# Layer 2 attention: value products in three steps of a round, projections in the other five

## The chip, the cores and the metric

The kernel runs on one NeuronCore of a Trainium2 chip. Its time is the device time of one launch in microseconds (us); lower is better. TensorE does the matrix products, VectorE and ScalarE work on their results in PSUM, GpSimd does small elementwise work, and SyncE's queue starts the loads. The engines run their own instruction streams in order and meet at semaphores.

## The reference, cut to what matters

Four layers, each a cross attention and a feed-forward part. The change touches the attention of layer 2 alone (8 batches, 256 queries, 512 keys, 16 heads of width 64, all in float32):

```python
def _L2_xattn_ref(x, context, mask, Wq, Wkv, Wout, b_out):
    HEADS, DIM_HEAD = 16, 64
    SCALE = DIM_HEAD ** (-0.5)
    q = x @ Wq.T
    k, v = jnp.split(context @ Wkv.T, 2, axis=-1)
    ...
    sim = jnp.einsum('bhid,bhjd->bhij', q, k) * SCALE
    sim = jnp.where(mask[:, None, None, :], sim, max_neg)
    attn = jax.nn.softmax(sim, axis=-1)
    out = jnp.einsum('bhij,bhjd->bhid', attn, v)
    return out.transpose(0, 2, 1, 3).reshape(B, Nq, HEADS * DIM_HEAD) @ Wout.T + b_out
x = x + _L2_xattn_ref(_layernorm(x, axis=-1), ctx_1024, mask_BxS2_bf1, ...)
```

## The kernel before, in words

`wide_attention` works on one batch at a time. The 16 heads are 8 pairs; a **round** is the 4 pairs of one half of the heads, so a batch has two rounds and the layer 16 (n = 2b + r). A round has eight **steps**, one for each block of 32 queries (QB = 8); a batch has steps s = 0 to 15, of which 0 to 7 are its first round and 8 to 15 its second. Below, "step two of a round" is the second one, s % 8 == 1.

In a step each engine does the following, in the order in which it is written for that engine:

- **TensorE** first issues the scores of the step that comes next (`scores`, L2007: 8 matmuls of a 64-row, 32-column tile, for two PSUM banks `s_ps`), after `max_ready` says that VectorE has read the scores before them. Then it fills banks for the step's **jobs** (`fill`): K, Q and V projections of this or the next batch (L1988, L1986, L1373), the turning XT of the normed input (L1982), and the output product OUT of the batch before (L1993, 8 matmuls). All jobs take turns in two PSUM banks, `ring` (RING = 2); a bank is refilled when `m.drained` says that it was emptied. Last come value products of the round before (`outputs`, L2023): 16 blocks of 32 keys, 8 matmuls each on 32-row, 64-column tiles, into `pv_ps`. With the last blocks go 8 matmuls (L2029) that spread the inverses of the softmax sums over the other half of `pv_ps`.
- **VectorE** takes the masked negative maxima of the scores of the next step (`maxima`, L1797, two), turns the probabilities of this step in 32x32 blocks (`turn_probs`, L1809, two), and in step one of a round multiplies `pv_ps` by its inverses (`normalise_outputs`, L1822) and inverts the sums of the round just ended (`invert_sums`, L1816). It also drains OUT jobs and takes their moments.
- **ScalarE** takes the exponentials for the next step (`exponentials`, L1926, two), in step one of a round copies the spread inverses from `pv_ps` to `o` (`copy_inv`, L1936), and then drains the step's K, Q, V and XT jobs from the ring (L1910, L1908, L1912, L1906).

Which job stands in which step is written in tables: `this_batch`, `next_batch`, `last_batch`, and `end_values` and `for_local` for the end of the last batch, where LOCAL jobs belong to the feed-forward part that follows. `blocks_of` says which of the 16 blocks of value products stand in which step of a round: before, seven of the eight steps have two or three. The value products of a round need `normalise_outputs` of the round before them (`m.pv_copied`), since they write the same `pv_ps`.

Of the kernel before, what the change touches and what calls it, by code (L numbers as in the profile page):

```python
# [41 lines left out]
class Ring:  # L42
# [15 lines left out]
    def bank(self, u, m):  # L58
        return self.banks[self.index(u, m)]
# [1436 lines left out]
class FirstLocal:  # L1496
# [3 lines left out]
    SHIFT, TURN, QK, V = 0, 1, 2, 2 + 2 * TPB  # L1500
# [123 lines left out]
def wide_attention(m):  # L1624
# [10 lines left out]
    QB, KB = S // BLK, KV // BLK  # L1635
# [4 lines left out]

    XT, Q, K, V, OUT, LOCAL = range(6)
    NQ, NV = NG // 2, 2 * CPB
    this_batch = {0: [(K, 4), (K, 5), (K, 6)], 1: [(K, 7)], 2: [(Q, 2)], 3: [(Q, 3)], 4: [(V, 0)], 5: [(V, 1)], 6: [(V, 2)], 7: [(V, 3)],
                  14: [(V, 4), (V, 5)], 15: [(V, 6), (V, 7)]}
    next_batch = {7: [(XT, 0)], 8: [(K, 0), (K, 1), (K, 2)], 9: [(K, 3)], 11: [(Q, 0)], 13: [(Q, 1)]}
    last_batch = {10: [(OUT, 0)], 12: [(OUT, 1)]}
    end_values = {8: [(V, 4), (V, 5)], 9: [(V, 6), (V, 7)]}
    for_local = {10: [0], 11: [1], 12: [2], 13: [3], 14: [4], 15: [5]}
    blocks_of = {1: range(0, 3), 2: range(3, 6), 3: range(6, 8), 4: range(8, 10), 5: range(10, 12), 6: range(12, 14), 7: range(14, 16)}

    def step_jobs(b, s):
        end = b + 1 == B
        jobs = [(f, b - 1, n) for f, n in last_batch.get(s, ()) if b > 0]
        own = end_values if end and s >= QB else this_batch
        jobs += [(f, b, n) for f, n in own.get(s, ()) if b > 0 or f == Q]
        jobs += [(f, b + 1, n) for f, n in next_batch.get(s, ()) if not end]
        if end:
            jobs += [(LOCAL, b, n) for n in for_local.get(s, ())]
        return jobs
    before = [(XT, 0, 0), (Q, 0, 0), (Q, 0, 1)]  # L1660
    steps = {(b, s): step_jobs(b, s) for b in range(B) for s in range(STEPS)}
    behind = [(LOCAL, B - 1, 6), (LOCAL, B - 1, 7), (OUT, B - 1, 0), (OUT, B - 1, 1)]
    jobs = before + [job for b in range(B) for s in range(STEPS) for job in steps[b, s]] + behind
    number = {job: n for n, job in enumerate(jobs)}

    with ExitStack() as ctx:
# [39 lines left out]
        def ahead(b, s):  # L1706
            return (b, s + 1) if s + 1 < STEPS else (b + 1, 0)

        with nc.Block() as block:
# [55 lines left out]
            def _(dve):  # L1765
# [92 lines left out]
                for b in range(B):  # L1858
                    for s in range(STEPS):
                        n = ROUNDS * b + s // QB  # L1860
                        if ahead(b, s)[0] < B:
                            maxima(*ahead(b, s))
                        turn_probs(b, s)
                        if s % QB == 0 and n >= 2:
                            normalise_outputs(n - 2)
                        if s % QB == 0 and n >= 1:
                            invert_sums(n - 1)
                        for job in steps[b, s]:
                            drain(job)
                        if s == 13 and b > 0:  # L1870
                            out_moments(b - 1)
                        if s == 15 and b > 0:
                            out_scale(b - 1)
                        if s == 6 and b + 1 < B:
                            convert_mask(b + 1)
                        if s == 10 and b + 2 < B:
                            scale(b + 2)
                        if b + 1 == B and s == 9:
                            dve.wait_ge(*m.out_normed.after(2 * TPB))
                            local.copy_half(dve)  # L1880
                            local.tables(dve)
                        if b + 1 == B and s == 14:
                            local.sum_squares(dve, 0)
# [14 lines left out]
            @block.scalar  # L1898
            def _(act):
                def drain(job):  # L1900
                    f, b, n = job
                    if f == OUT:
                        return
                    act.wait_ge(*full(job))
                    if f == XT:
                        ins = act.activation(xnT[b % 2][:], bank(job)[:, 0:S], ACT.Copy)  # L1906
                    if f == Q:
                        ins = act.activation(q[:, 2 * n:2 * n + 2, :].rearrange("p g s -> p (g s)"), bank(job)[:], ACT.Copy, scale=hd ** -0.5)  # L1908
                    if f == K:
                        ins = act.activation(kT[:, n, :], bank(job)[:], ACT.Copy)  # L1910
                    if f == V:
                        ins = act.activation(first.place_values(n), bank(job)[:], ACT.Copy)  # L1912
                    if f == LOCAL:
                        ins = local.drain(act, n, bank(job))
                    ins.then_inc(drains(job), 1)
                    if f == LOCAL and n in (local.QK + 1, local.QK + 3):
                        local.square(act, (n - local.QK) // 2, empty_local)

                def exponentials(b, s):
                    r, qb = divmod(s, QB)  # L1920
                    if qb == 0 and ROUNDS * b + r >= ROUNDS:
                        act.wait_ge(*m.sums_inverted.after(ROUNDS * b + r - 1))
                    for w in range(2):
                        n = 2 * s + w
                        act.wait_ge(*m.max_ready.after(UNITS * b + n + 1))
                        act.activation(probs[n % 4][:], probs[n % 4][:], ACT.Exp, bias=nmax[:, b % 2, n:n + 1], scale=-1.0,  # L1926
                                       accum_out=sums[:, r, w, qb:qb + 1]).then_inc(m.probs_ready.sem, 1)

                def copy_inv(n):

                    b, r = divmod(n, ROUNDS)
                    act.wait_ge(*m.pv_done.after(n + 1))
                    if b >= 1:
                        for j in range(TPB):
                            act.wait_ge(*full((OUT, b - 1, j)))
                    act.activation(o[:, NC * r:NC * (r + 1), :], pv_ps[:, :, S:2 * S], ACT.Copy).then_inc(m.inv_copied.sem, 1)  # L1936

                for job in before:
                    drain(job)
                exponentials(0, 0)  # L1940
                for b in range(B):
                    for s in range(STEPS):
                        n = ROUNDS * b + s // QB
                        if ahead(b, s)[0] < B:
                            exponentials(*ahead(b, s))
                        if s % QB == 0 and n >= 2:
                            copy_inv(n - 2)
                        for job in steps[b, s]:
                            drain(job)
                copy_inv(LAST - 1)  # L1950
                for job in behind[0:TPB]:
                    drain(job)
                copy_inv(LAST)
# [1616 lines left out]
```

## Time and profile before

| | |
|---|---|
| median of 3 runs | 1759.72 us (1755.17 to 1760.15) |
| the profiled execution | 1760.41 us, its span 1758.5 us |
| mean granted TensorE clock | 0.926 |
| TensorE busy (PE) | 1535.7 us, 87% |
| VectorE busy (DVE) | 1303.6 us, 74% |
| ScalarE busy (ACT) | 1032.9 us, 59% |
| GpSimd busy (POOL) | 569.5 us, 32% |

The span runs from the first to the last instruction of one execution; the other 1.9 us of that execution lie around it. Busy shares are averages over parts with different limits. Layer 2 attention lies between about 484 and 1006 us of the span. In the rows, PE is TensorE, PEld its weight loads, DVE VectorE, ACT ScalarE. A float32 matmul gives two records, so that 8 matmuls stand as x16.

### The profile page before, as it was taken

To read this page: it belongs to the slowest core of one execution; us is meant where nothing else is said; L and a number is where in the kernel's file an instruction comes from. 1 tells how busy PE (TensorE), PEld (TensorE's weight loads), DVE (VectorE), ACT (ScalarE), POOL (GpSimd) and SP (SyncE) were. 2 spreads that over 40 slices of the span, in tenths; PEclk is the share of its full clock that TensorE was granted. 3 is DMA by queue.
4 is the path that set the end of the run, shared out by engine and by line. 5 is a ranking of instruction groups with operands and counts; after the bars stand their busy time and mean duration, and the time that the engine had idled before them with its cause. 6 is when DMAs were issued, how large, how long until landed. Compare 5 with 4: busy or idle time off the path is not lost. (4 is left out here: it accounts for less than half of the span.)

```text
span 1758.5 us, 44254 instructions
## 1 busy us (share of the span) xinstructions
PE 1535.7 (87%) x16764; PEld 804.3 (46%) x16764; DVE 1303.6 (74%) x3513; ACT 1032.9 (59%) x2227; POOL 569.5 (32%) x618
## 2 busy tenths in 40 slices
PE   5886999997669999999999899979799896999976
PEld 3532344433424444444554556655466652333333
DVE  5636778885878777677777789956899666799847
ACT  2331666665846555556555389854689631777764
POOL 0306656521010000000000289915799303342210
PEclk9895999998869999999999899999999985899997
DMA  5124333301010000000000000010100002322100
GB/s 167 34 31 134 76 80 67 66 14 49 1 38 3 8 2 9 8 3 9 28 3 3 8 1 1 0 40 9 48 1 0 1 14 74 55 43 50 30 2 24
DMA packets 60284, 54.21 MB, mean 31 GB/s; under 512 B 9610, under 2 KB 52798, under 8 KB 59974
## 3 DMA queue, kind: packets, MB, share of 16 engines
q1 hardware_dynamic: 59238, 51.32, 12.1%
q8 instruction: 123, 2.02, 0.5%
q14 instruction: 59, 0.48, 0.1%
q10 hardware_dynamic: 864, 0.39, 0.1%
HBM read 30.59 MB, written 1.05 MB: 18 GB/s over the span
## 5 line engine op out<-in xcount | busy, mean ns | idle before, releaser
L1926 ACT ACTIVATE probs_l2x<-probs_l2x,nmax_l2x 128x512 f32<-128x512 f32 x256 | 182.8, 715 | 193.5 <-DVE nmax_l2x L1797 193.5
L1797 DVE CUSTOM_DVE_ANT_0 probs_l2x<-s_ps_l2x,mask_b_l2x 128x512 f32<-128x512 f32 x256 | 166.6, 689 | 120.5 <-PE s_ps_l2x L2007 120.1
L1072 DVE CUSTOM_DVE_ANT_0 junk_l1x<-s_ps_l1x,mask_b_l1x 128x512 f32<-128x512 f32 x256 | 166.3, 687 | 50.3 <-PE s_ps_l1x L1273 46.0
L1075 DVE TENSOR_REDUCE nmax_l3x<-s_ps_l3x 128x1 f32<-128x512 f32 x256 | 163.7, 683 | 33.6 <-PE s_ps_l3x L1273 31.9
L1134 ACT ACTIVATE pT_l1x<-st_ps_l1x 128x1024 f32<-128x1024 f32 x128 | 131.2, 1025 | 79.9 <-PE st_ps_l1x L1258 79.5
L1809 DVE STREAM_TRANSPOSE pT_l2x<-probs_l2x 128x512 f32<-128x512 f32 x256 | 166.4, 688 | 0.0
L2007 PE MATMUL s_ps_l2x<-kT_l2x_first,q_l2x 64*32 64x512 f32 x2048 | 147.5, 634 | 11.3 <-DVE nmax_l2x L1797 10.5
L2023 PE MATMUL pv_ps_l2x<-pT_l2x,v_l2x_first 32*64 32x256 f32 x4096 | 137.7, 385 | 2.6 <-issue 2.6
L1740 POOL TENSOR_TENSOR spread_l2x<-inv_l2x,consts 128x512 f32<-128x512 f32 x16 | 17.6, 1101 | 324.5 <-DVE inv_l2x L1816 324.5
L2618 POOL TENSOR_TENSOR rn_l2a_first<-ssc_l2a_first,consts 128x16 f32<-128x16 f32 x28 | 109.1, 3897 | 20.2 <-DVE ssc_l2a_first L2645 20.0
L2788 ACT ACTIVATE probs_l2a<-minus_s_l2a,nmax_l2a 128x128 f32<-128x128 f32 (+1 forms) x256 | 106.1, 424 | 9.5 <-DVE nmax_l2a L2693 9.5
L2574 POOL TENSOR_TENSOR v_l2x_first<-kT_l2x_first,tb_l2a_first 128x256 f32<-128x256 f32 x112 | 104.0, 960 | 5.2 <-ACT kT_l2x_first L2756 4.6
L2023 PEld LDWEIGHTS pv_ps_l2x<-pT_l2x,v_l2x_first 32*64 32x64 f32 x4096 | 79.9, 131 | 51.4 <-issue 37.2
L2693 DVE CUSTOM_DVE_ANT_0 minus_s_l2a<-s_ps_l2a,consts 128x128 f32<-128x128 f32 (+1 forms) x256 | 67.3, 317 | 31.3 <-PE s_ps_l2a L2906 27.8
L1273 PE MATMUL s_ps_l3x<-kT_l3x_first,q_l3x 51*128 51x512 bf16 x192 | 75.3, 435 | 15.1 <-DVE nmax_l3x L1075 8.2
L1285 PE MATMUL pv_ps_l1x<-pT_l1x,v_l1x 128*32 128x256 f32 x1024 | 81.2, 391 | 1.0 <-ACT o_l1x L1142 0.9
L1134 ACT ACTIVATE v_l2x_first<-st_ps_l3x 128x1024 f32<-128x1024 f32 x64 | 65.2, 1024 | 24.3 <-PE st_ps_l3x L1258 24.3
L1134 ACT ACTIVATE kT_l2x_first<-st_ps_l3x 128x1024 f32<-128x1024 f32 x64 | 65.3, 1024 | 20.8 <-PE st_ps_l3x L1258 20.1
L1245 PE MATMUL st_ps_l1x<-maskT_b_l1x,consts_bf 128*128 128x512 bf16 x256 | 77.4, 384 | 0.0
L1273 PE MATMUL s_ps_l1x<-kT_l1x_first,q_l1x 48*128 48x512 bf16 x192 | 66.3, 417 | 11.6 <-DMA q_l1x<-parts_l1x_first 8.1
L1258 PE MATMUL st_ps_l3x<-q_l3x,kT_l3x_first 54*128 54x256 bf16 x384 | 65.7, 284 | 0.0
L2945 PE MATMUL t_ps_l2a<-consts,probs_l2a 128*128 128x128 f32 x384 | 56.6, 284 | 4.7 <-ACT probs_l2a L2788 4.4
(531 smaller groups left out, 3574.9 us busy)
## 6 DMA issues: line engine op xcount, KB each, us to landing
mask_i_l1x<-in_mask SPq DMA_DIRECT2D x8, 512.0 KB, 4.2
maskT_i_l1x<-in_mask_t SPq DMA_DIRECT2D x8, 512.0 KB, 4.9
kT_l1x_first<-parts_l1x_first SPq DMA_DIRECT2D x60, 64.0 KB
kT_l3x_first<-parts_l3x_first SPq DMA_DIRECT2D x60, 64.0 KB
q_l1x<-parts_l1x_first SPq DMA_DIRECT2D x90, 32.0 KB
q_l3x<-parts_l3x_first SPq DMA_DIRECT2D x90, 32.0 KB
ctxT_l0x<-in_ctxT SPq DMA_DIRECT2D x9, 256.0 KB, 3.1
rows_l0x<-in_ctx SPq DMA_DIRECT2D x9, 256.0 KB, 4.2
```

Of the source, the lines that this page charges most:

```text
L1072: dve.tensor_tensor_reduce(out=junk[w][:], in0=s_ps[w][:], in1=mask_b[b % 2][:, j, :], scale=-1.0, scalar=3e38, op0=ALU.add, op1=ALU.min, ...
L1075: dve.tensor_reduce(to, s_ps[w][:], AX.X, ALU.max, negate=True).then_inc(m.s_drained[w].sem, 1)
L1134: act.activation(pT[t % 4][:, :, 2 * j:2 * j + 2, :].rearrange("p w c t -> p w (c t)"), st_ps[j][:], ACT.Exp)\
L1273: pe.matmul(s_ps[w][:], q[b % NST][rows, p, j * P:(j + 1) * P], kT[b % NST][rows, p, :], start=True, stop=True)\
L1797: dve.tensor_tensor_reduce(out=probs[n % 4][:], in0=s_ps[w][:], in1=mask_b[b % 2][:], scale=-1.0, scalar=3e38, op0=ALU.add, op1=ALU.min, a ...
L1809: dve.transpose(pT[r][:, w, :, BLK * qb:BLK * (qb + 1)], probs[unit % 4][:].rearrange("p (k t) -> p k t", t=BLK))\
L1926: act.activation(probs[n % 4][:], probs[n % 4][:], ACT.Exp, bias=nmax[:, b % 2, n:n + 1], scale=-1.0, accum_out=sums[:, r, w, qb:qb + 1]). ...
L2007: ins = pe.matmul(s_ps[w][BLK * c:BLK * (c + 1), :], q[rows, g, BLK * qb:BLK * (qb + 1)], kT[rows, g, :], start=True, stop=True)
L2023: pe.matmul(pv_ps[hd * w:hd * (w + 1), c, 0:S], v[BLK * c:BLK * (c + 1), r, kb, hd * w:hd * (w + 1)], pT[r][BLK * c:BLK * (c + 1), w, kb, ...
L2574: eng.tensor_tensor(other[j][:, w, :, to], qk[:, j, w, :, of], tb[:, w, j, to].unsqueeze(1).to_broadcast([P, NH, 32]), ALU.mult).then_inc( ...
L2618: pool.tensor_tensor(rn[:, cols], ssc[:, cols], k["minus_half"][:, 0:2 * NH], ALU.pow).then_inc(m.powers_ready.sem, 1)
L2788: act.activation(probs[n % (2 * DEEP)][:, cols], minus_s[n % (2 * DEEP)][:, cols], ACT.Exp, bias=nmax[:, u, TPB * n + j:TPB * n + j + 1], ...
```

## The change

The tables are written anew. Value products stand in steps four, six and eight of a round, with five, five and six blocks. Projections stand in the other steps, mostly two at a time, so that no step has three K jobs. V banks 6 and 7 of a batch move to step 0 of the batch after it. OUT jobs move from steps 10 and 12 to 13 and 14, and their moments from step 13 to 14. On ScalarE a step's drains stand ahead of `copy_inv`; on VectorE `normalise_outputs` moves from step one of a round to step two.

```diff
-    this_batch = {0: [(K, 4), (K, 5), (K, 6)], 1: [(K, 7)], 2: [(Q, 2)], 3: [(Q, 3)], 4: [(V, 0)], 5: [(V, 1)], 6: [(V, 2)], 7: [(V, 3)],
-                  14: [(V, 4), (V, 5)], 15: [(V, 6), (V, 7)]}
-    next_batch = {7: [(XT, 0)], 8: [(K, 0), (K, 1), (K, 2)], 9: [(K, 3)], 11: [(Q, 0)], 13: [(Q, 1)]}
-    last_batch = {10: [(OUT, 0)], 12: [(OUT, 1)]}
-    end_values = {8: [(V, 4), (V, 5)], 9: [(V, 6), (V, 7)]}
+    this_batch = {1: [(K, 4), (K, 5)], 2: [(K, 6), (K, 7)], 4: [(Q, 2), (Q, 3)], 6: [(V, 0), (V, 1)], 8: [(V, 2), (V, 3)],
+                  14: [(V, 4)], 15: [(V, 5)]}
+    after_batch = {0: [(V, 6), (V, 7)]}
+    next_batch = {7: [(XT, 0)], 9: [(K, 0), (K, 1)], 10: [(K, 2), (K, 3)], 12: [(Q, 0), (Q, 1)]}
+    last_batch = {13: [(OUT, 0)], 14: [(OUT, 1)]}
+    end_values = {8: [(V, 2), (V, 3)], 9: [(V, 4), (V, 5)], 10: [(V, 6), (V, 7)]}
...
-    blocks_of = {1: range(0, 3), 2: range(3, 6), 3: range(6, 8), 4: range(8, 10), 5: range(10, 12), 6: range(12, 14), 7: range(14, 16)}
+    blocks_of = {3: range(0, 5), 5: range(5, 10), 7: range(10, 16)}
...
         jobs += [(f, b, n) for f, n in own.get(s, ()) if b > 0 or f == Q]
+        jobs = [(f, b - 1, n) for f, n in after_batch.get(s, ()) if b > 1] + jobs
...
-                        if s % QB == 0 and n >= 2:
+                        if s % QB == 1 and n >= 2:
                             normalise_outputs(n - 2)
...
-                        if s == 13 and b > 0:
+                        if s == 14 and b > 0:
                             out_moments(b - 1)
...
+                        for job in steps[b, s]:
+                            drain(job)
                         if s % QB == 0 and n >= 2:
                             copy_inv(n - 2)
-                        for job in steps[b, s]:
-                            drain(job)
```

TensorE, batch 3, its first round from step 0 on. Before (`s_ps` scores, `ring` jobs, `pv_ps` value products):

```order
L2007 MATMUL s_ps_l2x<-kT_l2x_first,q_l2x 32x512 x8
L1988 MATMUL ring_l2x<-ctxT_l2x,wk_l2x_first 128x512 x3
L2007 MATMUL s_ps_l2x<-kT_l2x_first,q_l2x 32x512 x8
L1988 MATMUL ring_l2x<-ctxT_l2x,wk_l2x_first 128x512
L2023 MATMUL pv_ps_l2x<-pT_l2x,v_l2x_first 64x256 x24
L2007 MATMUL s_ps_l2x<-kT_l2x_first,q_l2x 32x512 x8
L1986 MATMUL ring_l2x<-xnT_l2x,wq_l2x_first 128x256 x2
L2023 MATMUL pv_ps_l2x<-pT_l2x,v_l2x_first 64x256 x24
L2007 MATMUL s_ps_l2x<-kT_l2x_first,q_l2x 32x512 x8
L1986 MATMUL ring_l2x<-xnT_l2x,wq_l2x_first 128x256 x2
L2023 MATMUL pv_ps_l2x<-pT_l2x,v_l2x_first 64x256 x16
L2007 MATMUL s_ps_l2x<-kT_l2x_first,q_l2x 32x512 x8
```

and in the changed kernel, from the same step:

```order
L2009 MATMUL s_ps_l2x<-kT_l2x_first,q_l2x 32x512 x8
L1373 MATMUL ring_l2x<-wv_l2x_first,ctxT_l2x_first 32x128 x32
L2009 MATMUL s_ps_l2x<-kT_l2x_first,q_l2x 32x512 x8
L1990 MATMUL ring_l2x<-ctxT_l2x,wk_l2x_first 128x512 x2
L2009 MATMUL s_ps_l2x<-kT_l2x_first,q_l2x 32x512 x8
L1990 MATMUL ring_l2x<-ctxT_l2x,wk_l2x_first 128x512 x2
L2009 MATMUL s_ps_l2x<-kT_l2x_first,q_l2x 32x512 x8
L2025 MATMUL pv_ps_l2x<-pT_l2x,v_l2x_first 64x256 x40
L2009 MATMUL s_ps_l2x<-kT_l2x_first,q_l2x 32x512 x8
L1988 MATMUL ring_l2x<-xnT_l2x,wq_l2x_first 128x256 x4
L2009 MATMUL s_ps_l2x<-kT_l2x_first,q_l2x 32x512 x8
L2025 MATMUL pv_ps_l2x<-pT_l2x,v_l2x_first 64x256 x40
```

The three K products of step 0 are gone: two V products of the batch before stand there, then two K in each of the next two steps. The first value products come in the fourth step, 40 matmuls at once, where before they began in the second with 24. Matmuls of one kind stand in fewer and longer pieces.

ScalarE at the same place, from the copy of the inverses (`o_l2x<-pv_ps_l2x`) on. Before:

```order
L1936 ACTIVATE o_l2x<-pv_ps_l2x 128x1024
L1910 ACTIVATE kT_l2x_first<-ring_l2x 128x512 x3
L1926 ACTIVATE probs_l2x,sums_l2x<-probs_l2x,nmax_l2x 128x512 x2
L1910 ACTIVATE kT_l2x_first<-ring_l2x 128x512
L1926 ACTIVATE probs_l2x,sums_l2x<-probs_l2x,nmax_l2x 128x512 x2
L1908 ACTIVATE q_l2x<-ring_l2x 128x512
L1926 ACTIVATE probs_l2x,sums_l2x<-probs_l2x,nmax_l2x 128x512 x2
L1908 ACTIVATE q_l2x<-ring_l2x 128x512
L1926 ACTIVATE probs_l2x,sums_l2x<-probs_l2x,nmax_l2x 128x512 x2
```

and in the changed kernel:

```order
L1914 ACTIVATE v_l2x_first<-ring_l2x 128x512 x2
L1938 ACTIVATE o_l2x<-pv_ps_l2x 128x1024
L1928 ACTIVATE probs_l2x,sums_l2x<-probs_l2x,nmax_l2x 128x512 x2
L1912 ACTIVATE kT_l2x_first<-ring_l2x 128x512 x2
L1928 ACTIVATE probs_l2x,sums_l2x<-probs_l2x,nmax_l2x 128x512 x2
L1912 ACTIVATE kT_l2x_first<-ring_l2x 128x512 x2
L1928 ACTIVATE probs_l2x,sums_l2x<-probs_l2x,nmax_l2x 128x512 x4
L1910 ACTIVATE q_l2x<-ring_l2x 128x512 x2
```

The copy now stands behind two V drains, no longer ahead of three K drains, and the K drains come two at a time behind the two pairs of exponentials that follow.

VectorE, the same steps. Before:

```order
L1797 ISA nmax_l2x 128x1
L1809 STREAM_TRANSPOSE pT_l2x<-probs_l2x 128x16x32 x2
L1822 TENSOR_TENSOR o_l2x<-pv_ps_l2x,o_l2x 128x1024
L1816 RECIPROCAL inv_l2x<-sums_l2x 128x16
L1797 ISA probs_l2x,nmax_l2x<-s_ps_l2x,mask_b_l2x 128x512
L1797 ISA nmax_l2x 128x1
L1797 ISA probs_l2x,nmax_l2x<-s_ps_l2x,mask_b_l2x 128x512
L1797 ISA nmax_l2x 128x1
L1809 STREAM_TRANSPOSE pT_l2x<-probs_l2x 128x16x32 x2
```

and in the changed kernel:

```order
L1799 ISA nmax_l2x 128x1
L1811 STREAM_TRANSPOSE pT_l2x<-probs_l2x 128x16x32 x2
L1818 RECIPROCAL inv_l2x<-sums_l2x 128x16
L1799 ISA probs_l2x,nmax_l2x<-s_ps_l2x,mask_b_l2x 128x512
L1799 ISA nmax_l2x 128x1
L1799 ISA probs_l2x,nmax_l2x<-s_ps_l2x,mask_b_l2x 128x512
L1799 ISA nmax_l2x 128x1
L1811 STREAM_TRANSPOSE pT_l2x<-probs_l2x 128x16x32 x2
L1824 TENSOR_TENSOR o_l2x<-pv_ps_l2x,o_l2x 128x1024
```

The multiplication of the outputs (`o_l2x<-pv_ps_l2x,o_l2x`) stood ahead of the reciprocal; it now stands one step later, behind two more maxima (the rows named ISA) and transposes, and ahead of the maxima of the step after.

## Rows read from the trace of the kernel before

**Rows 1.** The page's first line.

```profile
span 1758.5 us, 44254 instructions
```

**Rows 2.** Busy time by window: batch 0, then single rounds of batches 2, 4, 4, 7, 7.

```profile
core 0: us, PE busy (x) PEld busy (x) DVE busy (x) ACT busy (x) POOL busy (x), PEclk, DMA share, GB/s
494.56:545.83 51.27, 42.23 (x554) 14.09 (x555) 40.47 (x101) 28.60 (x74) 1.77 (x2) 0.77 0.01 2
638.48:672.69 34.21, 32.39 (x584) 16.62 (x576) 23.68 (x61) 18.20 (x45) 1.76 (x2) 0.95 0.02 4
736.16:765.40 29.24, 27.41 (x554) 12.79 (x546) 21.92 (x51) 18.08 (x45) 1.73 (x2) 1.00 0.03 10
765.40:797.97 32.57, 30.74 (x584) 16.44 (x577) 23.69 (x61) 18.22 (x45) 1.75 (x2) 1.00 0.02 4
921.60:952.05 30.45, 28.62 (x553) 12.77 (x545) 21.45 (x50) 17.70 (x44) 1.05 (x1) 0.94 0.01 2
952.05:984.37 32.32, 28.91 (x568) 15.78 (x561) 25.57 (x68) 19.95 (x43) 4.65 (x3) 1.00 0.01 3
```

**Rows 3.** TensorE's timeline, batch 4, steps 8 and 9: start, duration, what.

```profile
765.40 1.09 PE L2007 MATMUL s_ps_l2x<-kT_l2x_first,q_l2x 64*32 64x512 f32 x16
766.42 1.98 PE L1988 MATMUL ring_l2x<-ctxT_l2x,wk_l2x_first 128*128 128x512 f32 x4
770.23 1.13 PE L1988 MATMUL ring_l2x<-ctxT_l2x,wk_l2x_first 128*128 128x512 f32 x2 [1.83 <-ACT kT_l2x_first L1910]
771.29 1.09 PE L2007 MATMUL s_ps_l2x<-kT_l2x_first,q_l2x 64*32 64x512 f32 x16
...
773.36 1.55 PE L2023 MATMUL pv_ps_l2x<-pT_l2x,v_l2x_first 32*64 32x256 f32 x48
```

**Rows 4.** ScalarE's timeline in the same step.

```profile
767.27 0.72 ACT L1926 ACTIVATE probs_l2x<-probs_l2x,nmax_l2x 128x512 f32<-128x512 f32 x1 [1.55 <-DVE nmax_l2x L1797]
...
768.69 1.00 ACT L1936 ACTIVATE o_l2x<-pv_ps_l2x 128x1024 f32<-128x1024 f32 x1
769.60 1.07 ACT L1910 ACTIVATE kT_l2x_first<-ring_l2x 128x512 f32<-128x512 f32 x2
```

**Rows 5.** Waits of TensorE, 484 to 1000 us: total, times, longest.

```profile
PE ring_l2x L1988 <- ACT kT_l2x_first L1910: 23.7, 13, 1.8
```

**Rows 6.** TensorE's timeline, batch 3, steps 11 to 13 and the start of 14.

```profile
720.64 1.09 PE L2007 MATMUL s_ps_l2x<-kT_l2x_first,q_l2x 64*32 64x512 f32 x16
721.66 2.05 PE L1993 MATMUL ring_l2x<-wo_l2x,o_l2x 128*128 128x128 f32 x16
723.64 1.12 PE L2023 MATMUL pv_ps_l2x<-pT_l2x,v_l2x_first 32*64 32x256 f32 x32
724.69 1.09 PE L2007 MATMUL s_ps_l2x<-kT_l2x_first,q_l2x 64*32 64x512 f32 x16
725.71 1.13 PE L1986 MATMUL ring_l2x<-xnT_l2x,wq_l2x_first 128*128 128x256 f32 x4
726.77 1.12 PE L2023 MATMUL pv_ps_l2x<-pT_l2x,v_l2x_first 32*64 32x256 f32 x32
727.82 1.09 PE L2007 MATMUL s_ps_l2x<-kT_l2x_first,q_l2x 64*32 64x512 f32 x16
728.84 1.96 PE L1373 MATMUL ring_l2x<-wv_l2x_first,ctxT_l2x 128*32 128x128 f32 x64
730.72 1.12 PE L2023 MATMUL pv_ps_l2x<-pT_l2x,v_l2x_first 32*64 32x256 f32 x32
```

**Rows 7.** VectorE's timeline, batch 4, step 8.

```profile
766.53 0.69 DVE L1797 CUSTOM_DVE_ANT_0 probs_l2x<-s_ps_l2x,mask_b_l2x 128x512 f32<-128x512 f32 x1 [1.35 <-PE s_ps_l2x L2007]
...
767.76 1.30 DVE L1809 STREAM_TRANSPOSE pT_l2x<-probs_l2x 128x512 f32<-128x512 f32 x2
769.73 1.23 DVE L1822 TENSOR_TENSOR o_l2x<-pv_ps_l2x,o_l2x 128x1024 f32<-128x1024 f32 x1 [0.67 <-ACT o_l2x L1936]
```

**Rows 8.** TensorE's timeline, batch 0, steps with nothing but scores.

```profile
509.92 1.09 PE L2007 MATMUL s_ps_l2x<-kT_l2x_first,q_l2x 64*32 64x512 f32 x16 [1.40 <-DVE nmax_l2x L1797]
512.42 1.96 PE L2007 MATMUL s_ps_l2x<-kT_l2x_first,q_l2x 64*32 64x512 f32 x16 [1.40 <-DVE nmax_l2x L1797]
515.87 1.96 PE L2007 MATMUL s_ps_l2x<-kT_l2x_first,q_l2x 64*32 64x512 f32 x16 [1.49 <-DVE nmax_l2x L1797]
```

## The prediction

> **What bounds the kernel now.** I read the page first for the span [rows 1], then the busy time of single rounds of the layer. In a round of the steady part TensorE is busy all but 1.83 us of its 29.24 or 32.57 us, VectorE 22 to 24, ScalarE 18 [rows 2]: the matrix stream is the bound, and what is saved there shows in the time. Its timeline shows where the 1.83 us are: in the first step of a round the third K product waits for a ring bank [rows 3]. ScalarE, which must empty that bank, is late for two reasons one behind the other: it does its two exponentials, and then the copy of the inverses, from 768.69 to the K drain at 769.60, which is 0.91 us of the wait [rows 4]. The list of waits counts 13 of these, 23.7 us [rows 5].
>
> Two further costs hide in busy time. The granted clock is full (2.4 GHz) in both rounds of batch 4, but 0.95 in the second of batch 2, which takes 34.21 against 32.57 us, 1.64 more [rows 2]; the time is lost in the step right behind such a bank wait, where the matmuls run at the lower level (1.2 GHz). I count four such falls in the layer: two in batch 2, one in batch 3, one in batch 7 (30.45 us at 0.94) [rows 2]. And each change of the kind of matmul costs something: 32 records of value products hold TensorE for 1.05 us from start to start, 48 are busy for 1.55 where 32 are for 1.12 [rows 3, 6], so a block of 16 records costs 0.43 and every piece 1.05 - 2 x 0.43 = 0.19 us on top.
>
> **The pieces, in start-to-start times.** Scores 1.02, OUT 1.98, one Q bank 1.06, a pair of V banks 1.88 [rows 6]. A pair of K banks is 1.98 busy less the 0.07 of overlap that other pieces show, 1.91 [rows 3]; a pair of Q banks I take as the same. Value products in the new sizes: five blocks 1.05 + 3 x 0.43 = 2.34, six blocks with the spread matmuls (as large as a block) 1.05 + 5 x 0.43 = 3.20. So the short steps of the new order take 1.02 + 1.88 or 1.91 = 2.9 us (steps 0, 1, 2, 4, 6, 8, 9, 10, 12), the value steps 3.4 to 5.4.
>
> **Does the other side keep up with 2.9 us?** From the start of a step's scores (A) VectorE starts the maxima at A + 1.13, is through at A + 2.36 and turned at A + 3.6, 2.45 us of work [rows 7]. The floor of this loop stands in the trace: with nothing else to do, scores follow each other every 2.50 us [rows 8]. So 2.9 leaves 0.4. ScalarE starts its exponentials at A + 1.87 and is through at A + 3.29 [rows 4], and a pair of drains takes 1.0 more. TensorE could refill a bank 0.63 us after its drain starts (769.60 to 770.23) [rows 3, 4], here A + 3.92, and the next step asks for it at A + 2.9 + 1.02 = A + 3.92: just in time, with no margin.
>
> **Term 1, the K wait: -23.8 and back 4.8.** All 13 waits of 1.83 go. In their place: in step 0 the copy now follows the two V drains, from A + 4.3 to 5.2. The exponentials of step 1, due at 2.9 + 1.87 = 4.77, start at 5.2; the K drain behind them at 6.62, so that its bank can be refilled at 7.25, where step 2 wants it at 2 x 2.9 + 1.02, about 6.85. That is 0.4 us of wait in step three of a round, in 12 rounds (both of batches 2 to 6, one each of 1 and 7): +4.8. The normalising, moved to step 1 behind the transposes, ends at about A + 7.6 and makes VectorE 0.65 late for the maxima of step 2, which are through at 8.9; TensorE, late itself by the 0.4, asks at 9.1. It costs nothing there; without that cover it would cost up to 0.2 a round. The value products that need it come in step 3: nothing.
>
> **Term 2, pieces.** Value products go from 14 pieces a batch to 6: 8 x 0.19 = 1.5. Joined Q and V banks save three more pieces, 0.5, and the third K product no longer restarts alone, twice 0.2. Together 2.4 in a batch of 61.81 (29.24 + 32.57). With term 1 (2 x 1.83, less 0.8) a batch saves 5.3, and batches 2 to 6 save 26.5. Batch 1 has no V banks in step 0 (2.5 by the floor instead of 2.9, and no late copy): 6.1.
>
> **Term 3, the clock.** Four falls of 1.64 follow a wait of 1.83. I take them as gone, since the waits that stay are 0.4: 4.9 in batches 2 and 3, the fourth in batch 7.
> The Trainium skill (TensorE: Matmul & The Clock Gate, "A second HAM failure mode: psum-queue depth-cycling") speaks against this: short idles between groups of matmuls that take turns in PSUM can by themselves make the clock fall and rise again. This trace has 9 of 13 longer waits with no fall, so I price it only as a rival.
>
> **Term 4, the ends.** Batch 7, first round: the wait 1.83, the fall 1.64, half a batch's pieces 1.3, less the new wait 0.4: -4.4, so 30.45 goes to 26.0. Its second round does one V pair more (+1.9), keeps a bank wait, and the first LOCAL job has to wait for two V drains behind late exponentials (about 1.3): 32.32 goes to 34.8, +2.5. The tail behind it is not touched. Batch 0 has few jobs: its 51.27 us ran at clock 0.77 [rows 2], its floor is 2.50 at full and 3.45 at low clock (512.42 to 515.87) [rows 8]; I take no change, between -4 and +3.
>
> OUT jobs and their moments only move (steps 13, 14 are long; VectorE has slack), the moments' power on GpSimd has a whole step; the load of the next context now starts one step later, with nine steps until it is asked for. Cost nothing.
>
> Sum: 26.5 + 6.1 + 4.9 + 4.4 - 2.5 = 39.4 saved. The profiled execution took 1760.4 (span 1758.5 plus 1.9 around it), within 0.7 of the median; 1760.4 - 39.4 = **1721**. A measurement of this kernel tells about 0.3% (5.3 us) from no change.
>
> **Rivals.**
> (a) *ScalarE's drains bind the short steps* (chance 0.25). For it: a refill at A + 3.92 when it is asked for at A + 3.92 leaves nothing, every late exponential is handed to the next drain pair, and five of eight steps are short. Against: the average, 18 us of ScalarE in 26. At 0.3 us more in four steps of 14 rounds it gives back 17: 1738.
> The Trainium skill (TensorEngine Tiling, "PSUM Bottleneck") has this as a rule, that after packing the PSUM copies may become the bottleneck; by it the second of these two times would be right.
> (b) *The clock falls behind the waits that remain*, once a round: 12 x 1.64 = 20 us given back, 1741. For it: falls follow waits; against: the waits are a quarter as long. Within (a)'s chance and time.
> (c) *Slower*: the clock stays low through the short steps (chance 0.06). Place: the short steps, in which scores and two banks share one matrix stream with the loop's wait. In batch 0 scores after scores run 1.96 long instead of 1.09 [rows 8]. A short step has three such parts, 3 x 0.87 = 2.6 us more. There are about 65 short steps; with 39.4 / 2.6 = 15 of them at low clock the gain is gone, from 17 it is slower. At two in each of 14 rounds: 28 x 2.6 = 73, 1794. Against: TensorE has no gap in most of them, and where it was as busy as this in batch 4 the clock held [rows 2].
> That the change does not do what it says can be left out: the order of instructions shows it.
>
> **Numbers.** Forecast 0.69 (1713 to 1733), (a) and (b) 0.25 (1733 to 1747), (c) 0.06, a third of it within 0.3%. The range 1711 to 1745 leaves out (c) and the worst of (a); its low end is the forecast without the 0.4 waits and with batch 0 at -4. Faster by over 0.3%: 0.93; within: 0.03; slower: 0.04.
>
> **What would show it.** Batch 4 in 56.5 us instead of 61.8; the wait for L1910's drain at most 0.5 each, in step three of a round; value products in pieces of 80 and 96 records, 2.3 us and 2.8; no round of batches 1 to 6 under clock 1.00. If short steps take over 3.1 us, (a) is right, and the timeline names a drain; if PEclk in the rounds is under 0.97, (b) or (c). I am wrong if waits of scores for `nmax` appear in steps 1 to 2 of every round.

## The result, and the profile after

The changed kernel takes 1717.86 us (median of 4 runs, 1715.15 to 1718.63) against 1759.93 for the kernel before (1755.17 to 1760.35): ratio 0.9764, 95% interval 0.9744 to 0.9784, or 42 us less. Forecast were 1721 us and a range of 1711 to 1745.

The page of the profiled execution (1715.15 us), its span and busy times:

```profile
span 1713.3 us, 44203 instructions
PE 1497.1 (87%) x16713; PEld 810.6 (47%) x16764; DVE 1301.8 (76%) x3513; ACT 1030.0 (60%) x2227; POOL 569.6 (33%) x618
```

TensorE's busy time is 39 us lower on this page (1535.7 to 1497.1), but the page also lacks 51 matmul records (x16713 for x16764), none of them in the layer; the same kernel with both edits of the last batch, profiled twice below, shows 1503.5 us with these records and 1494.3 without. So some 9 of the 39 us are missing records, and the comparison is made inside the layer, where all records are there: TensorE is busy 471.0 us before and 444.7 after, 26 us less, and the rest of the gain is waiting. The other engines' busy time changed by 3 us at most.

Busy time by window of the changed kernel, to be laid beside [rows 2]: batch 0, the two rounds of batch 4, the second round of batch 7, and the tail of the layer.

```profile
core 0: us, PE busy (x) PEld busy (x) DVE busy (x) ACT busy (x) POOL busy (x), PEclk, DMA share, GB/s
491.13:541.68 50.55, 37.93 (x555) 14.06 (x555) 41.45 (x102) 29.35 (x77) 1.78 (x2) 0.83 0.01 2
710.28:736.63 26.35, 26.05 (x554) 13.74 (x546) 21.68 (x51) 18.06 (x44) 1.73 (x2) 1.00 0.05 12
736.63:766.67 30.04, 29.80 (x584) 17.20 (x576) 23.51 (x61) 17.91 (x43) 1.76 (x2) 1.00 0.01 3
905.37:942.70 37.33, 31.82 (x632) 18.63 (x625) 25.62 (x67) 20.62 (x44) 4.65 (x3) 0.95 0.01 3
942.70:963.72 21.02, 14.95 (x309) 13.04 (x309) 15.16 (x28) 2.11 (x3) 6.45 (x4) 0.92 0.01 2
```

Batch 4 takes 26.35 + 30.04 = 56.39 us instead of 61.81 [rows 2]. Batches 2 to 6 all take 56.38 or 56.39; before, batches 2 and 3 took 65.05 and 63.47 with their falls of the clock. The second round of batch 7 got longer, 37.33 against 32.32 [rows 2].

The first round of batch 4 on TensorE, which answers to [rows 3] (start, duration, what):

```profile
710.28 1.09 PE L2009 MATMUL s_ps_l2x<-kT_l2x_first,q_l2x 64*32 64x512 f32 x16
711.30 1.95 PE L1373 MATMUL ring_l2x<-wv_l2x_first,ctxT_l2x 128*32 128x128 f32 x64
713.19 1.09 PE L2009 MATMUL s_ps_l2x<-kT_l2x_first,q_l2x 64*32 64x512 f32 x16
714.21 1.98 PE L1990 MATMUL ring_l2x<-ctxT_l2x_first,wk_l2x_first 128*128 128x512 f32 x4
716.12 1.09 PE L2009 MATMUL s_ps_l2x<-kT_l2x_first,q_l2x 64*32 64x512 f32 x16
717.49 1.98 PE L1990 MATMUL ring_l2x<-ctxT_l2x_first,wk_l2x_first 128*128 128x512 f32 x4 [0.28 <-ACT kT_l2x_first L1912]
719.40 1.09 PE L2009 MATMUL s_ps_l2x<-kT_l2x_first,q_l2x 64*32 64x512 f32 x16
```

and on ScalarE, which answers to [rows 4]:

```profile
712.15 0.72 ACT L1928 ACTIVATE probs_l2x<-probs_l2x,nmax_l2x 128x512 f32<-128x512 f32 x1 [3.08 <-DVE nmax_l2x L1799]
712.87 0.71 ACT L1928 ACTIVATE probs_l2x<-probs_l2x,nmax_l2x 128x512 f32<-128x512 f32 x1
713.58 1.06 ACT L1914 ACTIVATE v_l2x_first<-ring_l2x 128x512 f32<-128x512 f32 x2
714.53 1.02 ACT L1938 ACTIVATE o_l2x<-pv_ps_l2x 128x1024 f32<-128x1024 f32 x1
715.44 0.72 ACT L1928 ACTIVATE probs_l2x<-probs_l2x,nmax_l2x 128x512 f32<-128x512 f32 x1
716.14 0.72 ACT L1928 ACTIVATE probs_l2x<-probs_l2x,nmax_l2x 128x512 f32<-128x512 f32 x1
716.85 1.08 ACT L1912 ACTIVATE kT_l2x_first<-ring_l2x 128x512 f32<-128x512 f32 x2
```

The steps are 2.91, 2.93 and 3.28 us long. ScalarE runs without a gap from 712.15 to the K drain at 716.85: exponentials, two V drains, copy, exponentials. The K product of step three could be issued from 717.14 (716.12 + 1.02) and starts at 717.49, 0.64 after that drain began. This is the only wait of the round; the step is 0.35 longer for it than the one before (0.29 in second rounds). The waits of TensorE from 484 to 970 us:

```profile
PE s_ps_l2x L2009 <- DVE nmax_l2x L1799: 15.9, 12, 1.5
...
PE ring_l2x L1990 <- ACT kT_l2x_first L1912: 3.0, 12, 0.3
...
PE ring_l2x L1539 <- ACT v_l2x_first L1914: 2.4, 1, 2.4
```

23.7 us in 13 waits [rows 5] became 3.0 us in 12. Of the 12 waits for `nmax`, 11 stand in batch 0 and the first step of batch 1, where steps have little else than scores, and one in the last batch (before: 10.5 us in 10). The wait of 2.4 for the first LOCAL job, L1539, is new.

From the first scores of the layer to the first matmul of the part behind it there were 514.78 us before (491.96 to 1006.74) and 475.18 after (488.54 to 963.72): 39.6 us less. By pieces:

| | before | after | saved | forecast |
|---|---|---|---|---|
| batch 0 from its second scores | 51.27 | 50.55 | 0.7 | 0 |
| batch 1 | 61.81 | 55.83 | 6.0 | 6.1 |
| batches 2 to 6 | 313.96 | 281.94 | 32.0 | 26.5 + 4.9 |
| batch 7, first round | 30.45 | 25.92 | 4.5 | 4.4 |
| batch 7, second round | 32.32 | 37.33 | -5.0 | -2.5 |
| the last round's products and the tail | 22.37 | 21.02 | 1.4 | 0 |
| sum | | | 39.6 | 39.4 |

The other 5.6 us by which the profiled spans differ (45.2 in all) lie in parts that the change does not touch: 3.4 ahead of the layer, the rest behind it. The span less the layer is 1235.6 to 1244.4 us in the 13 traces of this document, so 5.6 is within what these parts vary by.

### The profile page after: what moved, and what is told of

Read it like the earlier page. It is cut to its first block and busy times, and to the rows that moved or that the text cites. A ratio compares the mean times of both kernels' runs of the same rounds, so it can differ in the third digit from the quotient of the medians.

```text
span 1713.3 us, 44203 instructions
## 1 busy us (share of the span) xinstructions
PE 1497.1 (87%) x16713; PEld 810.6 (47%) x16764; DVE 1301.8 (76%) x3513; ACT 1030.0 (60%) x2227; POOL 569.6 (33%) x618
## 3 DMA queue, kind: packets, MB, share of 16 engines
HBM read 30.59 MB, written 1.05 MB: 18 GB/s over the span
## 5 line engine op out<-in xcount | busy, mean ns | idle before, releaser
L2025 PE MATMUL pv_ps_l2x<-pT_l2x,v_l2x_first 32*64 32x256 f32 x4096 | 122.3, 379 | 2.5 <-issue 2.5
L2025 PEld LDWEIGHTS pv_ps_l2x<-pT_l2x,v_l2x_first 32*64 32x64 f32 x4096 | 90.0, 131 | 39.2 <-issue 15.3
L1245 PE MATMUL st_ps_l1x<-maskT_b_l1x,consts_bf 128*128 128x512 bf16 x215 | 68.1, 383 | 4.7 <-issue 3.2
L2009 PEld LDWEIGHTS s_ps_l2x<-kT_l2x_first,q_l2x 64*32 64x32 f32 x2048 | 23.6, 106 | 79.4 <-DVE nmax_l2x L1799 46.0
```

Of the source, the lines that this page charges most:

```text
L2009: ins = pe.matmul(s_ps[w][BLK * c:BLK * (c + 1), :], q[rows, g, BLK * qb:BLK * (qb + 1)], kT[rows, g, :], start=True, stop=True)
L2025: pe.matmul(pv_ps[hd * w:hd * (w + 1), c, 0:S], v[BLK * c:BLK * (c + 1), r, kb, hd * w:hd * (w + 1)], pT[r][BLK * c:BLK * (c + 1), w, kb, ...
```

## The experiments

There are eleven runs: nine new kernels, one of them twice, and the changed kernel once more. They fall in three groups, and the time of the kernel before, measured with each group, was 1758.66, 1757.62 and 1756.99; totals of different groups are compared by their ratio to it. Even these ratios move: the changed kernel gave 0.9764 at first and 0.9806 in the third group, 7 us apart. So terms of a few us are read from the traces and not from totals. A batch of the changed kernel at full clock is 56.39.

### Where the copy stands on ScalarE (copy_first)

```diff
                             exponentials(*ahead(b, s))
-                        for job in steps[b, s]:
-                            drain(job)
                         if s % QB == 0 and n >= 2:
                             copy_inv(n - 2)
+                        for job in steps[b, s]:
+                            drain(job)
```

> The changed kernel with ScalarE's order undone: the copy of the inverses again ahead of the step's drains. Theory (the order of ScalarE's work sets when a ring bank comes free): the V drains of step one of a round start at A + 4.2 instead of A + 3.3, so the first K bank of step two can be refilled at A + 4.83 where it is wanted at A + 3.92. A wait of 0.9 us appears in step two of a round and the one of 0.25 in step three goes: 0.65 us in each of about 13 rounds, +8.5 us over the changed kernel, near 1726. Rival (the tables alone made the gain, with never more than two banks a step the order of drains is hidden): within 2 us of the changed kernel, 1718.

Measured: 1724.72 us, ratio 0.9813 (0.9790 to 0.9837). TensorE's timeline of batch 5, steps 0 to 2, and the whole batch by window:

```profile
776.38 1.96 PE L1373 MATMUL ring_l2x<-wv_l2x_first,ctxT_l2x_first 128*32 128x128 f32 x64
778.26 1.09 PE L2009 MATMUL s_ps_l2x<-kT_l2x_first,q_l2x 64*32 64x512 f32 x16
780.18 1.98 PE L1990 MATMUL ring_l2x<-ctxT_l2x,wk_l2x_first 128*128 128x512 f32 x4 [0.83 <-ACT v_l2x_first L1914]
782.10 1.09 PE L2009 MATMUL s_ps_l2x<-kT_l2x_first,q_l2x 64*32 64x512 f32 x16
```

```profile
775.36:832.92 57.56, 55.78 (x1130) 30.93 (x1123) 45.38 (x112) 35.97 (x87) 3.50 (x4) 1.00 0.03 7
```

The expected wait is there, a step earlier than the one it replaces: 57.56 is 1.17 more than 56.39, 0.6 a round, where 0.65 was expected; the wait in step three is gone (2.93). In 12 rounds that makes about 7 us, which is what the place of the copy is worth with these tables.

### Where the multiplication stands on VectorE (norm_one)

```diff
-                        if s % QB == 1 and n >= 2:
+                        if s % QB == 0 and n >= 2:
                             normalise_outputs(n - 2)
```

> The changed kernel with the multiplication by the inverses back in step one of a round on VectorE. Theory: it waits there for ScalarE's copy, which now ends at A + 5.3, and holds back the maxima of step two until A + 6.6 where they were due at A + 4.0. TensorE then waits about 2 us for nmax ahead of the scores in step three, and the K drains are late by 0.4 more: 2.2 us in each of 14 rounds, +31 us, near 1749, and up to 10 more if the clock falls behind these waits. Rival (VectorE has 2 us of slack a round, the place of the multiplication does not matter as long as it is done by step four): 1718 to 1722.

Measured: 1760.33 us, ratio 1.0010 (0.9998 to 1.0021). This one line gives back the whole gain. VectorE's timeline in batch 4, steps 0 and 1, and TensorE's:

```profile
735.37 1.23 DVE L1824 TENSOR_TENSOR o_l2x<-pv_ps_l2x,o_l2x 128x1024 f32<-128x1024 f32 x1 [1.64 <-ACT o_l2x L1938]
...
736.67 0.63 DVE L1799 CUSTOM_DVE_ANT_0 probs_l2x<-s_ps_l2x,mask_b_l2x 128x512 f32<-128x512 f32 x1
```

```profile
737.98 1.09 PE L2009 MATMUL s_ps_l2x<-kT_l2x_first,q_l2x 64*32 64x512 f32 x16 [1.99 <-DVE nmax_l2x L1799]
739.40 3.68 PE L1990 MATMUL ring_l2x<-ctxT_l2x_first,wk_l2x_first 128*128 128x512 f32 x4 [0.33 <-ACT kT_l2x_first L1912]
```

VectorE stands 1.64 us before the multiplication, and the scores of step three wait 1.99 for its maxima. The wait is what was expected, 2.1 us a round (5.00 against 2.93 for step two, and 0.05 in the next) or 29 us. Falls of the clock came on top, a little more than the 10 us allowed for: in 8 rounds of the 14 the K pair behind this wait ran wholly or in part at the lower clock, as here (3.68 for the pair that takes 1.98 at full clock), which costs 1.3 to 1.7 us each, about 12 us. The first theory stands; the rival, that the slack of the round hides the place, falls.

### Three K banks in one step (three_k)

```diff
-    this_batch = {1: [(K, 4), (K, 5)], 2: [(K, 6), (K, 7)],
+    this_batch = {1: [(K, 4), (K, 5), (K, 6)], 2: [(K, 7)],
...
-                  9: [(K, 0), (K, 1)], 10: [(K, 2), (K, 3)],
+                  9: [(K, 0), (K, 1), (K, 2)], 10: [(K, 3)],
```

> The changed kernel with K banks dealt out as before the change, three in one step and one in the next (steps two and three of a round), all else as changed. Theory (with a ring of two, a third job in a step waits for ScalarE whatever stands ahead of the drain): the third K product is wanted at 5.7 us from the round's start and its bank is free at 7.25, a wait of 1.55 plus 0.19 for starting alone, less the 0.25 that goes: 1.5 us in 13 rounds, +19 us, near 1737; each fall of the clock behind such a wait adds 1.6, at the old share of 4 in 13 about 6 more, 1743. Rival (the old wait was the copy's 0.91 and little else): at most 0.5 a round, 1718 to 1724.

Measured: 1742.33 us, ratio 0.9905 (0.9885 to 0.9926). TensorE's timeline in batch 5, step 1, the batch by window, and the list of waits:

```profile
788.52 1.98 PE L1990 MATMUL ring_l2x<-ctxT_l2x,wk_l2x_first 128*128 128x512 f32 x4
791.80 1.12 PE L1990 MATMUL ring_l2x<-ctxT_l2x,wk_l2x_first 128*128 128x512 f32 x2 [1.30 <-ACT kT_l2x_first L1912]
```

```profile
784.60:844.26 59.66, 56.38 (x1130) 30.80 (x1122) 45.34 (x112) 36.17 (x87) 3.49 (x4) 1.00 0.03 7
```

```profile
PE s_ps_l2x L2009 <- DVE nmax_l2x L1799: 20.8, 26, 1.5
PE ring_l2x L1990 <- ACT kT_l2x_first L1912: 17.1, 14, 1.3
```

A batch costs 3.27 more, 1.6 a round. The wait for the bank is 1.30 and not 1.55, but the step behind it, with one K bank left, comes down to the floor of 2.50 and waits for `nmax` there (the 14 further waits in the list against the changed kernel's 12). The third job makes most of the wait, but not all of it. TensorE's timeline has it as 0.93 in the first two rounds that have it, and 1.23 to 1.30 in the twelve later ones, where the V drains and the copy of the step before run up to the exponentials and make them late; 0.92 is also what is left in before_drains_first below, with no copy ahead. So the copy still holds 0.3 to 0.4 us from a step away. In batches 1 to 7 no round up to the first of batch 7 had a fall of the clock: the total sits above 1737 without the expected 6 us of falls. The layer is 22.6 us longer than in the changed kernel, 21.1 of it in these 13 rounds.

### The price of a piece (five_pieces)

```diff
-    blocks_of = {3: range(0, 5), 5: range(5, 10), 7: range(10, 16)}
+    blocks_of = {3: range(0, 3), 4: range(3, 5), 5: range(5, 8), 6: range(8, 10), 7: range(10, 16)}
```

> The changed kernel with the value products of a round in five pieces (3, 2, 3, 2 and 6 blocks in steps four to eight) instead of three. Nothing else moves; the short steps with Q and V pairs grow by two blocks, steps four and six shrink by two. Theory (every piece costs 0.19 us on TensorE): 2 more pieces in each of 15 rounds, 0.38 a round, +5.5 us, near 1723.5, with no new wait. Rival (the 0.19 is only a way of showing the ends of matmuls, or is hidden by the short steps' wait for VectorE): 0 to 1 us.

Measured: 1721.94 us, ratio 0.9798 (0.9781 to 0.9815). A batch by window:

```profile
772.00:829.31 57.31, 56.61 (x1131) 30.29 (x1123) 45.11 (x112) 35.98 (x87) 3.50 (x4) 1.00 0.03 7
```

0.92 us more a batch for four more pieces, 0.23 each where 0.19 was expected; TensorE's busy time grew by 0.76 of it (55.85 to 56.61), which is 0.19 a piece. The rest is a short wait for `nmax` in a step that lost two blocks. The price is real, and not only a way of showing the ends: from start to start, taking two blocks from a step saves 0.86 or 0.87, and adding a piece of two costs 1.05.

### Drains ahead of the copy, alone (before_drains_first)

```diff
--- the kernel before
                             exponentials(*ahead(b, s))
-                        if s % QB == 0 and n >= 2:
-                            copy_inv(n - 2)
                         for job in steps[b, s]:
                             drain(job)
+                        if s % QB == 0 and n >= 2:
+                            copy_inv(n - 2)
```

> The kernel before with one part of the change alone: ScalarE drains a step's jobs ahead of the copy of the inverses; tables and VectorE's order as before. Theory (the parts need each other): the third K product can start 0.91 earlier, but the copy now ends at about A + 6.4 and VectorE's multiplication, still in step one, at 7.6; the first value products, still in step two, wait for it by 0.6, so 0.3 us a round is left of the 0.91. With the falls of the clock that followed the waits of 1.83 gone, 4 + 6 us: between 1749 and 1756. Rival (the order of ScalarE's work is worth its 0.91 a round by itself): -12 and -6, near 1741.

Measured: 1751.15 us, ratio 0.9966 (0.9956 to 0.9976). TensorE's timeline of steps 0 and 1 of batch 5, VectorE's multiplication, and the batch by window:

```profile
797.78 1.12 PE L1988 MATMUL ring_l2x<-ctxT_l2x,wk_l2x_first 128*128 128x512 f32 x2 [0.92 <-ACT kT_l2x_first L1910]
...
801.81 1.55 PE L2023 MATMUL pv_ps_l2x<-pT_l2x,v_l2x_first 32*64 32x256 f32 x48 [0.83 <-issue]
```

```profile
800.49 1.23 DVE L1822 TENSOR_TENSOR o_l2x<-pv_ps_l2x,o_l2x 128x1024 f32<-128x1024 f32 x1 [2.97 <-ACT o_l2x L1936]
```

```profile
793.86:855.66 61.80, 58.30 (x1130) 29.52 (x1122) 45.30 (x112) 36.29 (x88) 3.49 (x4) 1.00 0.03 7
```

The K wait is halved, 0.92 for 1.83 (the copy's 0.91 is gone), and the value products wait 0.83 for the multiplication, which in turn waited 2.97 for the copy. The batch takes 61.80 us against 61.81: a wait was moved, and nothing gained, where 0.3 a round was expected. The 6 us that the total shows are the clock: in the trace no round up to the first of batch 7 had a fall, where the kernel before has four (these 13 rounds took 399.7 us for 406.2), and the granted clock of the ten executions is 0.930 to 0.935 where the kernel before, beside them, has 0.927 to 0.931. So this part of the change needs value products that start late; that it also needs the multiplication out of VectorE's way is what norm_one shows.

### The end of the last batch (tables_later, end_spread, both_ends, both_again)

The wait of 2.4 us at L1539 had two possible makers: the four V banks drained just before, and VectorE, where seven small operations (the copy of half the shifted input and the six rotation tables, 1.1 us in step 9) come right behind the moved multiplication.

```diff
                             local.copy_half(dve)
+                        if b + 1 == B and s == 11:
                             local.tables(dve)
```

> The changed kernel, with the seven rotation tables of the feed-forward part, which VectorE makes in step 9 of the last batch (1.1 us), moved to step 11; the copy ahead of them stays. Theory: in step 9 they come on top of the moved multiplication and hold back the maxima, the exponentials and then the V drains, for which the first LOCAL job waits 2.4 us. Without them that wait is 1.5, and the fall of the clock behind it may go: 1 to 2.6 us less than the changed kernel, 1715 to 1717. Rival (the wait is set by the four V banks in steps 9 and 10 alone): no change.

```diff
-    end_values = {8: [(V, 2), (V, 3)], 9: [(V, 4), (V, 5)], 10: [(V, 6), (V, 7)]}
+    end_values = {8: [(V, 2), (V, 3)], 9: [(V, 4), (V, 5)], 10: [(V, 6)], 12: [(V, 7)]}
```

> The changed kernel with the last V bank of the last batch moved from step 10 to step 12, where TensorE otherwise runs at the floor of 2.50; all else as changed. Theory: the first LOCAL job of step 10 then takes the ring bank that was drained a step earlier, and the wait of 2.4 us goes; the scores behind it wait for the maxima until about 1.1 later than the bank would allow. 2.5 us for the wait, 1.6 for the fall of the clock, 0.55 back in step 12: 3.6 less than the changed kernel, near 1714. Rival (VectorE, late by the multiplication and the tables, binds there and not the bank): at most 1 us less.

> Both edits of the last batch together: the last V bank in step 12, the tables in step 11. Theory (the bank first, then VectorE's tables bind): 4.6 us less than the changed kernel, near 1713, the lowest of all. Rival (one of them alone takes all there is): as end_spread, within 0.5.

Measured: tables_later 1719.68 us, ratio 0.9789 (0.9774 to 0.9804); end_spread 1717.18, 0.9775 (0.9760 to 0.9790); both 1714.05, 0.9747 (0.9729 to 0.9764). The totals of the first two cannot be told from the changed kernel, and both lie above what was expected (1715 to 1717 and 1714); the traces can tell why. The second round of batch 7 takes 34.84 us with the tables later, 34.78 with the V bank spread, and 33.83 with both, against 37.33. Of tables_later:

```profile
917.27 0.67 PE L1539 MATMUL ring_l2x<-y_l2a_first,consts 128*128 128x256 f32 x2 [1.50 <-ACT v_l2x_first L1915]
```

(The tables are six; the seventh operation, the copy, stayed.) The wait went from 2.44 to 1.50, as expected. The fall of the clock behind it is gone too, but that cannot be put down to the edit: three_k and five_pieces have the same wait (2.45 and 2.44) with no fall, and five_pieces' second round of batch 7 took 35.71. Of end_spread:

```profile
918.88 1.09 PE L2009 MATMUL s_ps_l2x<-kT_l2x_first,q_l2x 64*32 64x512 f32 x16 [0.95 <-DVE nmax_l2x L1799]
920.66 0.63 PE L1545 MATMUL ring_l2x<-consts,hb_l2a_first 128*128 128x128 f32 x4 [0.69 <-ACT hb_l2a_first L1555]
```

Here the bank wait is gone, and the next two in line show: the maxima, 0.95, and the drain of the LOCAL job, 0.69. So it gave 2.6 and not 3.6. With both edits the first of these is gone and the second stays, and they gave 3.5 and not 4.6.

What the first two gave was mostly lost again right behind that round. The value products of the last round, in the changed kernel and in tables_later:

```profile
942.70 7.17 PE L2025 MATMUL pv_ps_l2x<-pT_l2x,v_l2x_first 32*64 32x256 f32 x256 [2.49 <-issue]
```

```profile
941.45 8.85 PE L2026 MATMUL pv_ps_l2x<-pT_l2x,v_l2x_first 32*64 32x256 f32 x256 [2.49 <-issue]
```

The same work behind the same gap of 2.49 took 1.7 us more, at the lower clock, in tables_later and in end_spread, and the tail of the layer 22.73 us in both, against 21.02 in the changed kernel and 21.04 with both edits. No run shows why it falls in one and not in the other.

> The changed kernel as it is, beside the two others of this call on one chip, since the edits at the ends are worth less than two calls differ by. 1717 to 1719, ratio 0.976.

> The kernel with both edits of the last batch once more, on the same chip as the changed kernel. The traces gave 3.5 us less for the second round of batch 7 (33.83 against 37.33): 3.5 less than the changed kernel, 1714. If the gain of the traces is taken back in the part that follows, 0.

Measured on one chip: the changed kernel 1718.96 us, ratio 0.9806 (0.9780 to 0.9832), where 0.976 was expected; both edits 1712.57, 0.9763 (0.9746 to 0.9780). The second round of batch 7 with both edits:

```profile
906.52:940.35 33.83, 30.40 (x633) 18.14 (x625) 25.60 (x67) 20.49 (x44) 4.64 (x3) 1.00 0.01 3
```

Both times this kernel had the lowest median of its group. The traces put 3.5 us down to the edits (the layer takes 471.69 us for 475.24); that the medians are 6.4 apart is more than that, and the intervals just touch.

### The clock at the start of the layer (early_q)

```diff
+        own = {1: [(Q, 2), (Q, 3)]} if b == 0 else own
-        jobs += [(f, b, n) for f, n in own.get(s, ()) if b > 0 or f == Q]
+        jobs += [(f, b, n) for f, n in own.get(s, ())]
```

> Both edits of the last batch, and the second pair of Q banks of batch 0 in step 1 instead of step 4. In the changed kernel the first five steps of batch 0 run at the lower clock (scores 1.96 long) until this pair is done. Theory: the clock rises with that work, so three steps earlier, 3 x 0.87 = 2.6 us less than both edits, 1711.5. Rival: the clock falls again in the three steps with scores alone that then follow, as it did in the kernel before at 512.42: no gain, up to 1.7 more.

The edit stands on top of the two edits of the last batch.

Measured: 1721.78 us, ratio 0.9802 (0.9784 to 0.9820). TensorE's timeline of batch 0, and the batch by window:

```profile
501.31 1.09 PE L2011 MATMUL s_ps_l2x<-kT_l2x_first,q_l2x 64*32 64x512 f32 x16
503.80 1.09 PE L2011 MATMUL s_ps_l2x<-kT_l2x_first,q_l2x 64*32 64x512 f32 x16 [1.41 <-DVE nmax_l2x L1800]
506.29 1.09 PE L2011 MATMUL s_ps_l2x<-kT_l2x_first,q_l2x 64*32 64x512 f32 x16 [1.40 <-DVE nmax_l2x L1800]
508.79 1.09 PE L2011 MATMUL s_ps_l2x<-kT_l2x_first,q_l2x 64*32 64x512 f32 x16 [1.40 <-DVE nmax_l2x L1800]
511.29 1.96 PE L2011 MATMUL s_ps_l2x<-kT_l2x_first,q_l2x 64*32 64x512 f32 x16 [1.40 <-DVE nmax_l2x L1800]
```

```profile
493.44:546.62 53.18, 40.99 (x555) 14.77 (x555) 41.64 (x102) 29.45 (x77) 1.77 (x2) 0.78 0.01 2
```

A miss, and the rival was right: the clock rose with the Q pair, three steps earlier than in the run of both edits, held for four steps, each with a gap of 1.4 behind its scores, and fell again. Four steps and a K pair then ran at the lower clock, where the kernel of both edits had no fall after its Q pair. Batch 0 takes 53.18 us against 50.59 in the run of both edits beside it. That is 2.6 of the 9.2 us between the two medians; the rest lies in parts that are the same in both.

## Why the prediction was right

**Term 1, the K wait.** All 13 waits went. In step three of a round 0.35 or 0.29 us stands in their place, in 12 rounds, some 3.8 in all where 4.8 was forecast. The walk along ScalarE was right in every step (V drains, copy, exponentials at their end, K drain); it was up to 0.1 too long because drains and exponentials follow each other a little closer than their rows' lengths. That VectorE is late for the maxima of step 2 without cost is borne out, and norm_one shows what it costs in the other place: 2.1 a round.

**Term 2, pieces.** 5.42 saved a batch are 3.66 for the waits, less 0.64 for the new ones, and a rest of 2.4, as forecast for the pieces; TensorE's busy time in batch 4 fell by 2.3 (58.16 to 55.85). five_pieces gives the price by itself, 0.19 of TensorE's busy time a piece.

**Term 3, the clock.** All falls in batches 1 to 6 went, 4.9 us; norm_one shows them coming back with waits of 2. The doubt drawn from the Trainium skill (TensorE: Matmul & The Clock Gate, "A second HAM failure mode: psum-queue depth-cycling"), that short idles between groups of matmuls can by themselves make the clock fall, is not borne out for the waits of 0.3 in this order, 12 without a fall; early_q does show such a fall, after four gaps of 1.4.

**Rivals.** (a), drains that bind the short steps, did not come: they run in 2.90 to 2.99 us, all but step three of a round with its 3.28 or 3.22. The equality of A + 3.92 on both sides held. (b) and (c) did not come either: batches 2 to 6 ran at a granted clock of 1.00.

**Term 4, the ends, was off, and the step is named:** "Its second round does one V pair more (+1.9), keeps a bank wait, and the first LOCAL job has to wait for two V drains behind late exponentials (about 1.3)". It cost 5.0 and not 2.5. The terms that it names come to 3.2; why the sum says 2.5 is not in its text. The V pair was 1.9, as said, and the bank wait kept went from 0.84 to 0.22. The wait of the LOCAL job was 2.44 and not 1.3: the seven operations that VectorE does in step 9 of the last batch come right behind the moved multiplication, and were not counted; with the six tables moved away it was 1.50. And behind the wait the clock fell (the window's 0.95), 1.5 us, which the prediction did not price. Of four traces with this wait two had the fall, so that part is chance. The tail, forecast at nothing, gave 1.4 by a higher clock (0.92 against 0.84), which the change did not aim at; in the 13 traces it took 21.0 us five times and 22.3 to 22.7 eight times. Batch 0 gave 0.7. These errors nearly cancel, and that is luck: the layer's 39.4 met 39.6 closer than its terms deserve.

The median moved 42 us, 2.7 more than forecast. That is inside the interval of the ratio (38 to 45 us), and less than what the parts outside the layer vary by.

## What to carry to other kernels

Where engines meet in a ring of two, cost a new order as a walk through each in-order engine, step by step, from the rows of the old one: what is asked for when, what is free when. An order is one decision in several places. Here the drain order alone moved a wait and gained nothing in a round at full clock, and left in its old place it cost 7 us of the 40; the multiplication in its old place gave back everything. (The new tables with both old orders did not run.) And when work is moved onto a step, look at that step in the odd iterations too (the last batch, with its guests from the next part), not in the steady one alone.

## What the runs showed of the hardware that was not expected

The falls of TensorE's granted clock within the rounds sorted themselves by the wait ahead of them. Behind waits of 1.93 to 1.99 us there were 8 in 13 (norm_one), behind 1.83 there were 4 in 13 (the kernel before); behind waits of 1.23 to 1.30 none in 12 (three_k), behind 0.6 to 0.9 none in 12 (copy_first) and none in 13 (before_drains_first). Each of the twelve cost 1.3 to 1.7 us. Wait length is not all of it. The wait of 2.44 in the last batch had a fall behind it in two traces of four, and the gap of 2.5 ahead of the last round's value products in six of 13; copy_first and tables_later had one short fall each at the start of a round, at no such wait (scores 1.39 and 1.52 long). And in batch 0 a gap of 1.4 ahead of each step's scores ended in a fall after four steps in early_q (511.29), but not in the changed kernel, which ran five steps of scores with gaps of 1.2 to 1.5 at full clock (509.09 to 519.32).

Waits that are merely shortened can so give more than their length: in before_drains_first, where the rounds at full clock did not change at all, the total still fell by 6 us. What decides a single fall stays open.
